# Rebuilt routings in a kernel of two expert layers around an attention block, and a later load of some second weights

## The chip, the cores and the metric

One core of one Trainium2 chip. The metric is the device time of one execution in microseconds. The kernel before was run three times: 213.69, 214.22 and 214.76, median 214.22. One further execution was profiled.

## What is computed

The input `x` holds 4 batches of 512 tokens of width 128, so 2048 tokens. Three steps follow each other, each on a layer-normalised `x`:

```python
x = x + 0.5 * ffn(layernorm(x))      # router + 8 experts, top 1
x = x + attn(layernorm(x))           # linear attention, then a table-gelu MLP of width 512
x = x + 0.5 * ffn(layernorm(x))      # the same experts again

def ffn(x):
    logits = x @ router_W + router_b                 # 8 experts
    probs  = softmax(logits); top1 = argmax(probs)
    h = relu(x @ W1[e] + b1[e])                      # 128 -> 512, e = top1
    y = h @ W2[e] + b2[e]                            # 512 -> 128
    return probs[top1] * y
```

The reference computes all experts for all tokens. The kernel computes only the chosen one.

## The kernel before, in words

**Routing.** A routing finds the expert of each token, gives each token a place in a list sorted by expert, and cuts the list into tiles of 128 rows. Each expert's part is rounded up to whole tiles, so there are at most `NT` = 23 tiles. A tile has a *code*, its expert times 16 (`TPE`) plus its number within the expert. The chain of the first routing, by line:

- SP (SyncE) loads `x` in four groups (L374), then `rw`, `rb`, `eb1r`, the second biases, all first weights (L379, 2048 KB) and the eight second weights, one DMA of 256 KB each (L381). It then issues four small loads of `gb` (L386). TensorE waits for `rw` and `rb` together (L1022) before it averages the router's weights.
- VectorE takes statistics (L1208, L1211) of each group. GpSimd makes `rstd` and, for groups 0 and 1, `shift` (`normaliser`, L497 to L512).
- TensorE turns `x` (L858), ScalarE copies it out (L655), TensorE multiplies by the centred router weights (L889). `pick` on VectorE (L1229 to L1245, seven instructions for two groups) makes the one-hot `oh`.
- Between and behind the two `pick`s VectorE normalises groups 2 and 3 (L1218, `renormalise`). ScalarE normalises groups 0 and 1 (L701) and stores all four groups to DRAM, `xn_scratch` (L706).
- `ranks` (L898 to L912) counts on TensorE; `route` on VectorE goes on: `hits` (L1272), `tcol` (L1274, L1276), `v` and `pos` (L1279 to L1283), `qf`, `steps`, `inv` (L1286 to L1289), `rf` (L1292), `code` (L1296), `inq` (L1299) and sixteen `inr` (L1258, `row_hits`). TensorE's part of it is `tile_list` (L919 to L923) and `sources` (L968). VectorE writes the result as `srcu` (L1264), the row number of each list place.
- GpSimd turns `code` into the list of experts `eid` (L554 to L556). SP and TensorE read the list into registers (L326, 23 registers each).
- GpSimd waits for the stores of `xn_scratch` and for `srcu`, then gathers each tile by an indirect DMA into `Xg` (L549).

**Experts.** For each tile SP copies the expert's first weights inside SBUF to `ewc_own` (L390, 322 KB). `load_weights(k)` for k of 3 and more waits until TensorE has turned tile k-4, or the first one. TensorE turns the tile (`turn`, L978), multiplies by the first weights (`up`, L985) and by the second (`down`, L1000). ScalarE applies the relu (L681), VectorE copies and adds (L1349, L1355). In the first layer the order on TensorE is turn 0, turn 1, up 0, and then for each tile k: turn k+2, up k+1, down k. All eight second weights are waited for (`w2_in`) before turn 0. From tile 8 on SP also stores results (L394) and loads one attention weight for each tile (L409).

**Second routing.** It is incremental: `pick(1, b)` and `place(b)` run batch by batch during the last MLP, and GpSimd scatters the rows with their statistics into `row_scratch` (L609, four DMAs for each batch). Before batch b's `rstd` (L501) GpSimd scatters two of the four parts of batch b-1. After the last batch come `hits`, `tcol` (L1331, L1333), `steps` (L1335), `inv` (L1336), `code` (L1339), the list of codes (L1340) and the list of experts (L1341 to L1343). SP and TensorE read the experts' list, ScalarE reads the first eight codes and loads eight tiles of rows (L332). SP reads the codes when it reaches tile 8; from there on it loads rows for tile k after `out_done` of tile k-8, the landing of its output store (L617, GpSimd).

**Warm-up products.** `keep_warm(n)` (L842) issues n products of ones on TensorE with no result that is used.

The list read and the row load are:

```python
def load_list(eng, table, most):
    return nc.values_load_multi_w_load_instructions(table, [eng.engine], min_val=0, max_val=most, ...)[1]
for k in range(NT):                     # SP, second layer
    if k == UNROLL:                     # 8
        sp.wait_ge(codes_ready, 1)
        codes = load_list(sp, lists[0:1, 1, :], CODES - 1)
        for g in range(NG):
            sp.wait_ge(scattered[g], 16 * GT)
```

## Time and profile before

| | |
|---|---|
| median of 3 runs | 214.22 us (213.69 to 214.76) |
| the profiled execution, own time | 215.13 us |
| its span on the core | 213.4 us |
| TensorE busy | 190.5 us, 89% |
| VectorE, ScalarE, GpSimd busy | 124.7, 107.5, 119.8 us |
| mean granted TensorE clock | 0.968 |
| DMA | 40.26 MB, mean 189 GB/s |

In the profile PE is TensorE's matmuls and PEld its weight loads, DVE is VectorE, ACT ScalarE, POOL GpSimd, SP SyncE; a q behind the name is the engine's queue, which issues DMAs and reads registers. All times in rows are microseconds from the start of the span, if not marked ns. PEclk is the granted TensorE clock as a share of full speed: 1.00 is 2.4 GHz, 0.50 is 1.2 GHz. TensorE's busy share holds the warm-up products.

### The profile page before, as it was taken

The page shows a single profiled execution, that of the slowest core. Times are in us where ns is not written, and L with a number is a line of the kernel's source. Part 1 is how long each engine was busy: PE and PEld are TensorE (multiplying, and loading weights), DVE is VectorE, ACT ScalarE, POOL GpSimd, SP SyncE. Part 2 cuts the span into 40 slices and gives each one's busy share as a digit, 9 for nine tenths or more (in the row PEclk, how much of TensorE's full clock was granted, in tenths as well). Part 3 has the DMA queues.
Part 4 walks back from the last instruction along what each step waited for, and adds up shares of the span by engine and source line. Part 5 has one row for each costly group of instructions (what it writes and reads, how often), then busy time and mean ns, then how long its engine had stood idle before and what let it go on. Part 6 is the DMA issues. An engine that isn't in the chain of part 4 may idle for free.

```text
span 213.4 us, 4550 instructions
## 1 busy us (share of the span) xinstructions
PE 190.5 (89%) x1414; PEld 159.3 (75%) x1414; DVE 124.7 (58%) x528; ACT 107.5 (50%) x316; POOL 119.8 (56%) x186
## 2 busy tenths in 40 slices
PE   5997839999999888888989999989698999899992
PEld 2763339999999876677775769679335999899991
DVE  4688811222222773988797674777433776677762
ACT  2630004665556479747878863510301666466670
POOL 7872277755586445743777531857770245355544
PEclk9998875999999999999999999999969999999999
DMA  5999688779996231299990000011119838586700
GB/s 160 228 388 342 170 286 318 226 249 327 264 285 187 59 80 37 77 418 416 415 420 20 2 3 0 27 40 43 40 54 324 305 103 283 182 278 203 258 25 0
DMA packets 29752, 40.26 MB, mean 189 GB/s; under 512 B 4229, under 2 KB 20392, under 8 KB 28704
## 3 DMA queue, kind: packets, MB, share of 16 engines
q1 hardware_dynamic: 23968, 33.58, 44.3%
q0 software_dynamic: 2496, 4.76, 8.7%
q10 hardware_dynamic: 3264, 1.62, 2.6%
q8 instruction: 12, 0.20, 0.4%
q14 instruction: 12, 0.10, 0.1%
HBM read 10.78 MB, written 14.46 MB: 118 GB/s over the span
## 4 chain that ended last, share of the span: by engine, by line
PE 54%; POOL 13%; DMA 11%; DVE 9%; issue 8%; ACT 2%; SPq 1%; POOLq 0%; DVEq 0%
PE bank L985 14%; PE bank L1000 13%; PE bank L1122 6%; PE bank L842 5%; PE bank L1138 5%; POOL xnT L570 5%; DMA xnT<-slot_scratch,posu 3%; DMA eqrq<-row_scratch 2%; PE bank L978 2%; POOL h L579 2%; DMA Xg<-xn_scratch,srcu 2%; DMA out_dram<-ysb,eqrq 2%; DMA rb<-in_L_ffn_router_b_dram 2%; POOL ew L627 1%; PE bank L889 1%
## 5 line engine op out<-in xcount | busy, mean ns | idle before, releaser
L681 ACT ACTIVATE hT<-bank,ewc_own 128x128 f32<-128x128 f32 x184 | 52.6, 369 | 63.8 <-PE bank L985 62.9
L985 PE MATMUL bank<-xT,ewc_own 128*128 128x128 f32 x368 | 50.8, 283 | 0.6 <-DVE xT L1349 0.6
L1000 PE MATMUL bank<-ew,hT 128*128 x368 | 49.6, 279 | 0.0
L985 PEld LDWEIGHTS bank<-xT,ewc_own 128*128 128x128 f32 x368 | 46.6, 198 | 1.5 <-issue 1.0
L1000 PEld LDWEIGHTS bank<-ew,hT 128*128 128x128 f32 x368 | 45.6, 195 | 0.4 <-issue 0.4
L617 POOL DMA_INDIRECT out_dram<-ysb,eqrq x23 | 22.5, 979 | 29.5 <-DVE ysb L1359 26.2
L549 POOL DMA_INDIRECT Xg<-xn_scratch,srcu x23 | 22.0, 957 | 15.3 <-PE bank L978 7.5
L842 PE MATMUL bank<-ones_bf 128*128 128x512 bf16 x83 | 25.8, 446 | 3.4 <-POOL ident L466 2.6
L1355 DVE TENSOR_TENSOR ysb<-bank,ewc_own 128x128 f32<-128x128 f32 x23 | 6.7, 290 | 28.9 <-PE bank L1000 28.8
L609 POOL DMA_INDIRECT row_scratch<-pay,posu x16 | 15.8, 987 | 10.9 <-DVE posu L1317 7.6
L570 POOL DMA_INDIRECT xnT<-slot_scratch,posu x16 | 15.4, 962 | 10.5 <-DMA slot_scratch<-ysb 6.7
L1349 DVE COPY xT<-bank 128x128 f32<-128x128 f32 x46 | 13.0, 283 | 8.9 <-PE bank L978 8.9
L842 PEld LDWEIGHTS bank<-ones_bf 128*128 128x128 bf16 x83 | 8.4, 115 | 12.7 <-issue 6.6
L978 PE MATMUL bank<-ident,Xg 128*128 128x128 f32 x46 | 13.2, 288 | 4.8 <-DMA Xg<-xn_scratch,srcu 3.3
L1138 PE MATMUL bank<-w,actT 128*128 128x128 f32 x128 | 16.3, 278 | 0.0
L1138 PEld LDWEIGHTS bank<-w,actT 128*128 128x128 f32 x128 | 15.1, 192 | 0.0
L1122 PE MATMUL bank<-h1T,w 128*128 128x512 f32 x32 | 14.4, 592 | 0.0
L776 ACT ACTIVATE actT<-ewc_own 128x512 f32<-128x512 int16 x16 | 9.3, 622 | 8.0 <-DVE ewc_own L1545 8.0
L1359 DVE SCALAR_TENSOR_TENSOR ysb<-bank,gate,ysb 128x128 f32<-128x128 f32 x23 | 8.1, 351 | 8.6 <-PE bank L1000 7.6
L978 PEld LDWEIGHTS bank<-ident,Xg 128*128 128x128 f32 x46 | 6.7, 147 | 6.2 <-DMA Xg<-xn_scratch,srcu 2.5
L1368 DVE TENSOR_SCALAR Xg<-eqrq 128x128 f32<-128x128 f32 x23 | 7.7, 339 | 6.3 <-DMA eqrq<-row_scratch 6.2
L1122 PEld LDWEIGHTS bank<-h1T,w 128*128 128x128 f32 x32 | 5.8, 190 | 5.7 <-issue 5.5
(226 smaller groups left out, 296.8 us busy)
## 6 DMA issues: line engine op xcount, KB each, us to landing
ewc_own<-ew SPq DMA_DIRECT2D x46, 322.0 KB, 4.0
row_scratch<-xn SPq DMA_DIRECT2D x8, 1024.0 KB, 10.6
ew<-in_L_ffn_W_dram SPq DMA_DIRECT2D x1, 2048.0 KB, 11.8
ew<-in_L_ffn_W_dram SPq DMA_DIRECT2D x8, 256.0 KB, 7.7
slot_scratch<-ysb SPq DMA_DIRECT2D x23, 64.0 KB, 2.6
eqrq<-row_scratch SPq DMA_DIRECT2D x15, 70.0 KB, 2.3
x<-in_L_attn_x_dram SPq DMA_DIRECT2D x4, 256.0 KB, 3.8
xn_scratch<-xn ACTq DMA_DIRECT2D x4, 256.0 KB, 6.9
```

Source lines behind the costliest of these rows:

```text
L549: g.indirect_dma_start(out=Xg[:, k % UNROLL, :], out_offset=None, in_=xn_scr, in_offset=bass.IndirectOffsetOnAxis(ap=srcu[:, k:k + 1], axis=0)
L570: g.indirect_dma_start(out=Yg[:, t, :], out_offset=None, in_=here, in_offset=bass.IndirectOffsetOnAxis(ap=posu[:, t:t + 1], axis=0)).then_ ...
L609: g.indirect_dma_start(out=row_scr, out_offset=bass.IndirectOffsetOnAxis(ap=posu1[:, t:t + 1], axis=0), in_=pay[:, t, :], in_offset=None). ...
L617: g.indirect_dma_start(out=out_rows, in_=ysb[:, k, :], in_offset=None, bounds_check=TOK - 1, oob_is_err=False, out_offset=bass.IndirectOff ...
L681: last = A(hT[:, t.slot, c * P:(c + 1) * P], up_bank(k, c)[:, c * P:(c + 1) * P], ACT.Relu, scale=0.5 if m else 1.0, bias=ewc[t.ahead][:, ...
L842: mm(bank[2][:, :], ones_bf[:, :], bc(ones_bf[:, :].unsqueeze(1), [P, 4, P]), start=True, stop=True)
L978: nc.tensor.transpose(bank[t.parity][:, 0:P], Xg[:, t.ahead, :], ident[:, :]).then_inc(xg_T, 1)
L985: last = mm(up_bank(k, c)[:, c * P:(c + 1) * P], ewc[t.ahead][:, c * P:(c + 1) * P], xT[:, t.slot, :], start=True, stop=True)
L1000: last = mm(bank[4 + t.parity][:, 0:D], hT[:, t.slot, c * P:(c + 1) * P], ew[:, bass.ds(e[k], 1), W2_AT + c * D:W2_AT + (c + 1) * D].squee ...
L1122: mm(hidden_bank(c)[:, :], w1[:, c * P:(c + 1) * P], h1T[:, b % 2, :], start=True, stop=True).then_inc(u_ps, 1)
L1138: last = mm(row_bank(b, j)[:, j * P:(j + 1) * P], actT[:, b % 2, c, j * P:(j + 1) * P], w2[:, c, :], start=c == 0, stop=c == FC - 1)
L1349: v.tensor_copy(xT[:, t.slot, :], bank[t.parity][:, 0:P]).then_inc(xT_ready, 1)
```

## The change

In words, by place:

- **Layout.** Partition p of `x` holds four neighbouring tokens of a batch, 2 KB in one piece of DRAM, where it held four tokens 128 apart. `xn_scratch`, `token1` and the token numbers in `pay` follow.
- **Front.** ScalarE's queue loads `rw` first of all; `rb` has a semaphore of its own, waited for by VectorE ahead of `pick`. ScalarE takes all four `xnT` first, then normalises groups 0, 1 and 3; GpSimd normalises group 2. VectorE normalises none and makes the four `shift`s.
- **First routing.** Constants that VectorE added are put into PSUM by TensorE ahead of time (`whole`, `add_step`, `tileid`, `ecapb`). Of the 16 `inr` VectorE makes 9, GpSimd 3 and ScalarE 4, in two instructions each. The expert list comes from an integer shift on VectorE. SP reads codes instead of experts and works out the expert in registers. TensorE reads its list before `sources`.
- **Weights.** SP issues five of the eight second weights in front, and the last three behind the first tile's `load_weights`. The wait for all eight moves to down 0. The four `gb` loads move behind the attention weights, at tiles 14 to 17.
- **Experts.** In both layers TensorE's order is turn 0, warm-up, up 0, turn 1.
- **Second routing.** The same in PSUM. One scatter instead of two goes ahead of the last `rstd`. SP reads all codes at the start; SP and ScalarE wait until TensorE has read its list (`experts_loaded`) before they issue DMAs. ScalarE loads five tiles of rows, SP the other three at tile 3.

```diff
-    x_v = x_d.rearrange("b (t p) d -> p (b t) d", p=P)
+    x_v = x_d.rearrange("b (p j) d -> p b j d", j=GT)
...
+        def load_w2(eng, experts):
+            for e in experts:
+                eng.dma_start(ew[:, e, W2_AT:EW]..., ew2_d[e, :, :]...).then_inc(w2_in, 16)
...
-            for e in range(NE):
-                sp.dma_start(ew[:, e, W2_AT:EW]..., ew2_d[e, :, :]...).then_inc(w2_in, 16)
+            load_w2(sp, range(NE - W2_LATE))
...
-            sp.wait_ge(eid_ready, 1)
-            experts = load_list(sp, eid[0:1, 0:NT], NE - 1)
+            sp.wait_ge(whole_ready, 1)
+            codes = load_list(sp, codei[0:1, 0:NT], NE * TPE - 1)
...
-                load_weights(t, experts[k])
+                load_weights(t, expert_of(codes[k]))
+                if k == 0:
+                    load_w2(sp, range(NE - W2_LATE, NE))
...
-            sp.wait_ge(list_ready, 1)
-            experts = load_list(sp, lists[0:1, 0, :], NE - 1)
+            sp.wait_ge(codes_ready, 1)
+            codes = load_list(sp, lists[0:1, 0:NT], CODES - 1)
             sp.wait_ge(b2_halved, 1)
+            sp.wait_ge(experts_loaded, 1)
...
-                if k == UNROLL:
-                    sp.wait_ge(codes_ready, 1)
-                    codes = load_list(sp, lists[0:1, 1, :], CODES - 1)
+                if k == FIRST:
                     for g in range(NG):
                         sp.wait_ge(scattered[g], 16 * GT)
+                    for n in range(SURE, UNROLL):
+                        load_rows(sp, Tile(n), codes[n])
...
+            for t in range(POOL_ROWS * GT, (POOL_ROWS + 1) * GT):      # GpSimd, POOL_ROWS = 2
+                last = g.tensor_scalar(xn[:, t, :], x[:, t, :], mv[:, t, 0:1], rstd[:, t, 0:1], ALU.subtract, ALU.mult)
+            last.then_inc(xn_by_pool, 1)
+            pool.wait_ge(rf_ready, 1)
+            for t in range(T - ROWS_BY_ACT - ROWS_BY_POOL, T - ROWS_BY_ACT):
+                g.tensor_scalar(inr[:, t, :], rowid[:, :], rf[:, t:t + 1], token1[:, t:t + 1], ALU.is_equal, ALU.mult
+                                ).then_inc(inr_by_pool, 1)
...
+                ahead_of = GT // 2 if b + 1 < B else 1
-                scatter_rows(b - 1, range(GT // 2))
+                scatter_rows(b - 1, range(ahead_of))
                 normaliser(LN_AT["m1", b] - 1)
...
-            take_xn(0, 0)
-            take_xn(0, 1)
+            for g in range(NG):
+                take_xn(0, g)
             renormalise(0)
-            take_xn(0, 2)
-            take_xn(0, 3)
             renormalise(1)
-            for g in range(BY_ACT):
-                store_xn(g)
+            store_xn(0)
+            store_xn(1)
+            renormalise(3)
+            store_xn(3)
+            store_xn(POOL_ROWS)
             exponentials()
-            for g in range(BY_ACT, NG):
-                store_xn(g)
+            row_hits()
...
+            act.wait_ge(experts_loaded, 1)
             for k in range(SURE):
                 load_rows(act, Tile(k), codes[k])
-            act.wait_ge(scattered[NG - 1], 16 * GT)
-            for k in range(SURE, UNROLL):
-                load_rows(act, Tile(k), codes[k])
...
-            keep_warm(8)
+            keep_warm(4)
             ranks()
+            tile_list()
             keep_warm(2)
-            tile_list()
-            keep_warm(WARM_ROUTE // 2)
-            sources()
-            keep_warm(WARM_GATHER // 2)
             pe.wait_ge(eid_ready, 1)
             e = load_list(pe, eid[0:1, 0:NT], NE - 1)
-            keep_warm(2)
-            pe.wait_ge(w2_in, 16 * NE)
+            sources()
+            keep_warm(10)
             experts(0, e)
...
-            keep_warm(5)
+            keep_warm(8)
             ranks1(NG - 1)
             tile_list1()
-            keep_warm(WARM_ROUTE // 2)
+            keep_warm(4)
             pe.wait_ge(list_ready, 1)
-            e = load_list(pe, lists[0:1, 0, :], NE - 1)
-            keep_warm(12)
+            e = load_list(pe, lists[0:1, NT:2 * NT], NE - 1)
+            mm(bank[2][:, 0:P], ones_bf[:, :], ones_bf[:, :], start=True, stop=True).then_inc(experts_loaded, 1)
+            keep_warm(8)
             experts(1, e)
...
             pick(0, 0, 2)
-            renormalise(2)
-            pick(0, 2, 2)
-            renormalise(3)
+            first_shift(2)
             dve.wait_ge(eb1_T, 1)
             v.tensor_copy(ew[:, :, B1_AT:B2_AT], bank[7]...).then_inc(ebias_ready, 1)
+            pick(0, 2, 2)
+            first_shift(3)
             route()
```

Both `code` chains on VectorE:

```diff
-                v.tensor_tensor(out=code[:, :], in0=bank[6][:, 0:NT], in1=tileid[:, :], op=ALU.add
-                                ).then_inc(code_ready, 1)
+                v.tensor_scalar(codei[:, :], bank[6][:, 0:NT], NE * TPE - 1.0, None, ALU.min).then_inc(whole_ready, 1)
+                dve.wait_ge(whole_ready, 1)
+                v.tensor_scalar(eid[:, :], codei[:, :], TPE_BITS, None, ALU.arith_shift_right).then_inc(eid_ready, 1)
...
-                link(v.tensor_tensor(out=code[:, :], in0=bank[6][:, 0:NT], in1=tileid[:, :], op=ALU.add))
-                v.tensor_scalar(lists[:, 1, :], code[:, :], CODES - 1.0, None, ALU.min).then_inc(codes_ready, 1)
-                link(v.tensor_scalar(eidf[:, :], code[:, :], 1.0 / TPE, 0.5 / TPE - 0.5, ALU.mult, ALU.add))
-                link(v.tensor_scalar(eidf[:, :], eidf[:, :], MAGIC, MAGIC, ALU.add, ALU.subtract))
-                v.tensor_scalar(lists[:, 0, :], eidf[:, :], NE - 1.0, None, ALU.min).then_inc(list_ready, 1)
+                link(v.tensor_scalar(codei[:, :], bank[6][:, 0:NT], NE * TPE - 1.0, None, ALU.min))
+                v.tensor_scalar(lists[:, NT:2 * NT], codei[:, :], TPE_BITS, None, ALU.arith_shift_right).then_inc(list_ready, 1)
+                v.tensor_scalar(lists[:, 0:NT], bank[6][:, 0:NT], CODES - 1.0, None, ALU.min).then_inc(codes_ready, 1)
```

## Rows read from the trace of the kernel before

**Rows 1.** The page: busy us of the engines, share of the span, instructions.
```profile
PE 190.5 (89%) x1414; PEld 159.3 (75%) x1414; DVE 124.7 (58%) x528; ACT 107.5 (50%) x316; POOL 119.8 (56%) x186
```

**Rows 2.** The chain that ended last: start, us, what.
```profile
3.50 3.57 DMA rb<-in_L_ffn_router_b_dram
...
12.63 1.11 DVE xn L1218 x4
...
19.57 3.49 PE bank L842 x8
...
26.46 3.70 DMA Xg<-xn_scratch,srcu
...
91.49 2.27 POOL h L579 x4
```

**Rows 3.** The timeline, first routing: start, us, engine, line.
```profile
7.36 1.65 ACT L701 ACTIVATE xn<-x,shift,rstd 128x128 f32<-128x128 f32 x4
...
10.94 0.23 DVE L1229 TENSOR_TENSOR lg<-bank,rstd 128x64 f32<-128x64 f32 x1 [0.66 <-DVE mv L1211]
...
16.46 0.15 DVE L1272 COPY hits<-bank 128x1 f32<-128x1 f32 x1
...
19.68 0.18 DVE L1296 TENSOR_TENSOR code<-bank,tileid 128x23 f32<-128x23 f32 x1
...
20.35 3.21 DVE L1258 TENSOR_SCALAR inr<-rowid,rf,token 128x128 f16<-128x128 f16 x14
...
23.84 0.18 DVE L1264 TENSOR_SCALAR srcu<-bank 128x23 uint32<-128x23 f32 x1 [0.28 <-PE bank L968]
...
24.91 1.25 POOL L549 DMA_INDIRECT Xg<-xn_scratch,srcu  x1 [3.53 <-DVE srcu L1264]
```

**Rows 4.** Line 326, the reads of a list into registers: ns min/median/max, starts.
```profile
L326 SPq TENSOR_LOAD <-lists x2: 2017/3934/5852, 157.5 to 167.2; - x2
L326 PEldq TENSOR_LOAD <-eid x1: 2282/2282/2282, 23.6 to 23.6; - x1
```

**Rows 5.** Windows of 2.5 us: busy by engine, granted clock, DMA share, GB/s.
```profile
17.50:20.00 2.50, 1.96 (x12) 0.83 (x11) 2.29 (x12) 0.00 (x0) 0.06 (x1) 0.90 1.15 341
22.50:25.00 2.50, 2.46 (x25) 1.25 (x23) 2.18 (x8) 0.00 (x0) 0.09 (x1) 0.92 0.84 206
...
32.50:35.00 2.50, 2.50 (x12) 2.50 (x13) 0.29 (x1) 1.44 (x6) 1.88 (x2) 0.50 1.03 373
```

**Rows 6.** Line 706, the stores of `xn_scratch`.
```profile
L706 ACTq DMA_DIRECT2D xn_scratch<-xn x4: 366/410/490, 10.1 to 16.5; - x4
...
DMA to landing us min/median/max: 6.6/6.9/7.4
```

**Rows 7.** Line 381, the second weights.
```profile
L381 SPq DMA_DIRECT2D ew<-in_L_ffn_W_dram x8: 1241/1733/3037, 6.1 to 20.1; - x8
```

**Rows 8.** The timeline, first layer: turn of tile 2, down of tile 0.
```profile
32.42 0.48 PE L978 MATMUL bank<-ident,Xg 128*128 128x128 f32 x1
...
34.39 1.92 PE L1000 MATMUL bank<-ew,hT 128*128 x8
```

**Rows 9.** The timeline, second routing and its first tile.
```profile
149.44 0.38 DVE L1613 BATCH_NORM_AGGREGATE pay<-stat 128x2 f32<-128x6 f32 x4
149.57 0.96 POOL L609 DMA_INDIRECT row_scratch<-pay,posu  x1 [0.31 <-issue]
...
157.32 0.18 DVE L1343 TENSOR_SCALAR lists<-eidf 128x23 int32<-128x23 f32 x1
...
159.67 7.50 SPq L390 DMA_DIRECT2D ewc_own<-ew  x8
...
163.18 0.97 PEld L985 LDWEIGHTS bank<-xT,ewc_own 128*128 128x128 f32 x8 [0.29 <-DMA ewc_own<-ew]
```

**Rows 10.** The chain that ended last, rows of tile 11.
```profile
177.83 4.97 DMA eqrq<-row_scratch
```

**Rows 11.** The waits from 163 us on: us in total, times, longest us.
```profile
DVE Xg L1368 <- DMA eqrq<-row_scratch: 2.5, 2, 1.7
```

More of the change, by code:

```diff
@@ L328, in load_list, with within, expert_of @@
                 skip_runtime_bounds_check_because="the engine that makes the table clamps all of it to this range")[1]
+        def within(value, most):
+            return nc.s_assert_within(value, min_val=0, max_val=most, skip_runtime_bounds_check_because=
+                                      "codes are clamped to 0 to 128, and 128 is taken as 127")
+        def expert_of(code):
+            return within(within(code - (code >> (TPE_BITS + 3)), NE * TPE - 1) >> TPE_BITS, NE - 1)
         def load_rows(eng, t, code):
```

292 lines of the change are left out of this document (164 added, 128 removed).

## The prediction

> **What bounds the kernel now.** I read the page first: TensorE is busy 89% of the span [rows 1], but that holds the warm-up products, so its share tells little. The chain of waits tells more. Through both expert layers it runs on TensorE, tile after tile, and the diff leaves that work alone. It leaves TensorE in the two routings. In the first the chain names `rb` as what ended the wait at 3.50 + 3.57 = 7.07 us, then VectorE's normalising, 1.11 us for four rows, then 3.49 us of warm-up products, then the gather of tile 1 [rows 2]. The warm-up products are no cause: they fill the time in which VectorE makes 14 `inr` in 3.21 us, the last ready at 23.56 [rows 3], and `sources` needs all of them. So the timeline of VectorE is the view to cost this change from. The stage ends with the gathers, of which tile 0's starts at 24.91 [rows 3], and TensorE runs without gaps from the turn of tile 2 at 32.42 [rows 8].
>
> In the second routing the first `up` starts at 163.18 and its wait was ended by the landing of the weights that SP issued at 159.67, 3.5 us before; SP issued them 2.2 us after the list's end at 157.50 [rows 9], and 2.0 us of that is the list read [rows 4].
>
> **First routing, part by part.** The profiled execution took 215.13, 0.91 over the median of 214.22; I work out differences on its rows and take them from the median.
>
> - Front: VectorE waited for `rw` and `rb`, which TensorE needed together. `rw` now goes first on ScalarE's queue. Also five warm-up products of 0.44 us (3.49 for eight [rows 2]) go ahead of the first turn instead of seven, 0.9 us. `pick` starts at 10.94 now [rows 3]; with four groups of statistics on end and two small shifts between them I get 9.8. Gain 1.1.
> - Between the `pick`s one normalising of 1.11 [rows 2] goes, a shift and the bias copy, some 0.2 each, come. Behind the second `pick` the other 1.11 and the copy go, but then the wait is TensorE's answer. `hits`, at 16.46 [rows 3], comes at 14.05: gain 2.4.
> - One instruction of `tcol` (0.14) and two warm-up products ahead of `tile_list` go; of VectorE's chain behind the ranks the addition of `ecap` (0.28, a quarter of the 1.11 in [rows 2], which has as many elements) and that of `steps` (0.15). The four constants come from TensorE, ahead of `oh`, where it idles. `code`, at 19.68 [rows 3], comes at 16.7: gain 3.0.
> - Ahead of `inq` there is one instruction more, 0.2: gain 2.8.
> - `inr`: VectorE makes 7 more, 7 x 0.23 (3.21 / 14) = 1.6 us, done at 19.3. GpSimd makes 3; its nearest row is 2.27 for four rows [rows 2], 0.57 each, done at 18.2 if nothing holds it. ScalarE makes 4 in 8 instructions; its nearest row is 1.65 for four [rows 3], 0.41 each. It comes free at 17.0, behind its third normalising, two stores and the exponentials, so 17.0 + 3.3 + 0.1 = 20.4. ScalarE's are the last. Against 23.56 the gain is 3.15.
> - TensorE's list read moves ahead of `sources`, and everything on TensorE queues behind it. It took 2.28 [rows 4]; from 17.1 it ends at 19.4, covered by ScalarE's `inr` by 1.0 us. GpSimd's three instructions for `eid` leave; nothing waits on them at the end.
> - `srcu` at 20.7 to 20.9 instead of 24.02; the gather's own start, 0.9 behind it [rows 3], stays.
> - The gather also needs the four stores. The last two now go out at 15.7 and 16.2, hardly earlier than the 16.5 of [rows 6], because group 3's shift is late and GpSimd needs 2.27 for group 2. With the landing of [rows 6], 7.4, the last would be there at 23.6: 2.8 late. Against that stand pieces of 2 KB instead of 512 B and 768 KB less in front of them, 2.2 us at 341 GB/s [rows 5]. I take 4.8 for the landing, 21.0, about even with `srcu`, and charge 0.15. Gather 0 starts at 21.9: **gain 3.0**, ends 1.0 and 4.0.
> - Second weights: five DMAs in front, three behind the first tile's weights. SP reads its list from 16.9 to about 19.0, then issues at 19.2 what it issued at 26.1; the three land some 4 us later, by 24.5. The gathers of tiles 0 to 2 run beside them as they ran beside weight loads, 3.70 for tile 1 [rows 2]. Cost 0 while the three land ahead of `down` 0, which was at 34.39 [rows 8] and would be at 30 to 31; past that each microsecond is lost. The four `gb` loads come at tiles 14 to 17, one DMA each on SP's queue, where the attention weights stood at tiles 8 to 13; nothing but the later attention waits for them: 0.
> - `up` 0 ahead of turn 1 fills a wait for the gather; the next wait, tile 2's gather, stays last: 0. From 32.50 to 35.00 TensorE ran at clock 0.50 [rows 5]. It will sit idle there again, so I take the same; if the clock stayed up, half of that stretch, 1.2 us, would come back.
>
> **Second routing.**
>
> - Statistics are done at 149.82, GpSimd's second scatter held it until 150.53 [rows 9]. With one scatter ahead, `rstd` starts 0.7 earlier, and `pick` with it. The moved scatters end where they did: they gate only tiles 5 and later.
> - One instruction in `tcol`, one in `steps` go (0.3), but the warm-up products between hold TensorE: 0.2.
> - The list needs three instructions fewer, about 0.8. SP waits for the codes, made last: ready 1.45 earlier than 157.50 [rows 9], 156.05. The read ends at 158.1. The added wait, `experts_loaded`, ends with TensorE's own read (ready 155.9, plus 2.3, plus one product), 158.4. SP's first weights go at 158.5 instead of 159.67, 1.15 earlier, and land 3.5 later at 162.0. Behind SP's wait stand all weights, behind ScalarE's the rows of tile 0: those go at 158.4, land about 2 later, with slack.
> - TensorE: 8 warm-up products from 158.4 take 1.8 us at full clock and 3.5 at the lower one, then turn and 2 more, so `up` 0 is free at 161 or 163.1. Gain 1.15 or 0.1; I take **0.9**.
> - Tiles 8 on: SP's second read took 5.85 [rows 4], from 167.2 to 173.05; tile 8's rows and weights could not go out before, and 9 to 11 crowded behind. Tile 11's rows landed after 4.97 [rows 10], and VectorE waited 2.5 us for rows in two waits [rows 11], of which the gaps on TensorE show about half, 1.3. The read is gone from there. The round trip of store and reload stays, so I take half of the 1.3: **0.6**, ends 0 and 1.3.
>
> Sum: 3.0 + 0.9 + 0.6 = 4.5, so 214.22 - 4.5 = **209.7 us**. Its own range is 207 to 212.
>
> **A rule beside a row.** 23 registers took 2.28 us [rows 4], 99 ns each, while the DMA share in that window was 0.84 and falling [rows 5]; the same read at a full share took 5.85, 254 ns each. The Trainium skill, Runtime: NRT & Kernel Launch, section Instruction fetch mechanics, states about 200 ns for each register. By that figure, as an estimate, the read would take 4.6, end at 21.7 and leave 1.2 of the 3.0, total 211.5; the reads of the second routing, all about 2.0, speak against it.
>
> **The rivals.**
>
> 1. *The slow list read.* At 17.1 the DMA engines may still be full: from 17.50 to 20.00 the share was 1.15 [rows 5]. For it: the one read made under full DMA took 5.85. Against: five DMAs in front, not eight, end some 2 us sooner. The read ends at 22.95, `sources` takes 0.9, `srcu` is at 24.1: the first routing gains nothing, the second its 1.5. Time 212.7.
> 2. *The stores decide.* The last lands at 23.6, as now, and gather 0 goes at 24.0. Gain 0.9 + 1.5: 211.8. For it: the landings of [rows 6], all alike whatever was ahead; against it: larger pieces.
> 3. *Nothing measurable.* Slow read, and TensorE at 0.50 through the first tiles of the second layer, as it has fewer warm-up products after a longer idle time; that costs about 0.9 for each `up` or `down`, half of the 1.92 that `down` 0 took at the lower clock [rows 8]; one of them and the lost head start of 0.3 take the 1.5 down to 0.3. 213.9.
> 4. *Slower: the late second weights hold down 0.* SP's read is slow (22.8), then the tile's weights and three DMAs, each as slow to issue as the slowest, 3.04 [rows 7]: issued by 32.8, and landing as late as a store did in that crowd, 7.4 [rows 6], 40.2. `down` 0 would start there instead of at 34.39 [rows 8]: 5.8 lost, 1.5 gained, 218.5. It decides from a landing at 37.0 on (34.39, the 1.5, and 1.1 more). Against it: the backlog that made those DMAs slow is gone by then.
>
> **How the numbers follow.** The forecast gets 0.58, the rivals 0.17, 0.12, 0.07 and 0.06. About 0.5%, 1.1 us, is what a measurement of this kernel can tell from no change. Faster: 0.58 + 0.12 and nearly all of rival 1, 0.16, so 0.86. Same: rival 3 and the rest of rival 1, 0.08. Slower: 0.06. The range leaves out rivals 3 and 4 and the best corner: upper end 213.1, rival 1 with the second routing's lower end; lower end 206.9, first routing 4.0, second 1.15 and 1.3, and part of the clock's 1.2.
>
> **What would show it.** In the changed profile `hits` near 14.0, `code` near 16.7, `srcu` near 20.8, the first gather near 21.9 and ended by `srcu` or a store; TensorE's list read near 2.3 us; turn of tile 2 near 29.4; the first weights of the second layer 1.15 sooner than now, counted from the end of batch 3's statistics; no list read behind tile 7. A list read of 4 us or more at 17, or a wait of `down` 0 for `ew`, would make the prediction wrong, and a lower clock in the second layer's first tiles would take the 0.9.

## The result and the profile after

| | before | after |
|---|---|---|
| median of 19 runs each | 213.41 us (212.25 to 214.82) | 215.74 us (213.52 to 219.59) |
| ratio | | 1.0064, 95% interval 1.0036 to 1.0092 |
| the profiled execution, own time and span | 215.13, 213.4 us | 214.22, 212.5 us |
| mean granted TensorE clock in it | 0.968 | 0.939 |

The change makes the kernel slower by 0.6%. The forecast was 209.7 us. The ratios here and below leave out runs that took over 1.5% more than the fastest of their kernel, which the medians keep (five of the changed kernel's 19 are such runs), so the medians lie 2.3 us apart and the ratio says 1.4 us. Note which executions the profiles show: that of the kernel before is slower than all 19 of its runs, that of the changed kernel is the fifth fastest of its 19. So the two traces, read side by side, show the change 0.9 us ahead, and the medians show it 2.3 us behind. The traces tell where time moved; only the medians tell how much is left.

The page of the changed kernel: busy us of each engine, and the granted clock in 40 slices.

```profile
PE 186.4 (88%) x1403; PEld 157.8 (74%) x1403; DVE 120.1 (57%) x512; ACT 112.2 (53%) x328; POOL 123.5 (58%) x187
...
PEclk9965578999999999999999999999966999999998
```

VectorE has 4.6 us less than in [rows 1], ScalarE and GpSimd 4.7 and 3.7 more, as planned. The clock row has a hollow of three slices at 6, 5 and 5, from 10.6 to 26.6 us.

Its timeline in the first routing (start, us, engine, line), to be laid beside [rows 3]:

```profile
13.37 3.15 POOL L568 TENSOR_SCALAR xn<-x,mv,rstd 128x128 f32<-128x128 f32 x4
14.26 0.16 DVE L1343 COPY hits<-bank 128x1 f32<-128x1 f32 x1 [0.31 <-PE bank L954]
15.67 1.21 ACTq L749 DMA_DIRECT2D xn_scratch<-xn  x2
17.72 2.59 POOL L573 TENSOR_SCALAR inr<-rowid,rf,token 128x128 f16<-128x128 f16 x3 [1.21 <-DVE rf L1357]
18.17 0.17 DVE L1362 TENSOR_SCALAR codei<-bank 128x23 int32<-128x23 f32 x1
19.03 1.65 ACT L760 ACTIVATE inr<-off_row,token,minus_token 128x128 f16<-128x128 f16 x4
20.79 0.57 SPq L405 DMA_DIRECT2D ewc_own<-ew  x1
21.41 1.80 SPq L364 DMA_DIRECT2D ew<-in_L_ffn_W_dram  x3
21.72 0.18 DVE L1335 TENSOR_SCALAR srcu<-bank 128x23 uint32<-128x23 f32 x1 [0.99 <-PE bank L1041]
23.26 1.25 POOL L591 DMA_INDIRECT Xg<-xn_scratch,srcu  x1 [1.46 <-issue]
28.51 0.33 PE L1051 MATMUL bank<-ident,Xg 128*128 128x128 f32 x1 [2.56 <-DMA Xg<-xn_scratch,srcu]
34.29 0.27 PE L1051 MATMUL bank<-ident,Xg 128*128 128x128 f32 x1
```

`hits` is 2.2 us earlier than before, the list of codes 1.5, `srcu` 2.1, gather 0 1.65. But gather 0 takes 5.2 us to land, and turn 0, at 28.51, is *later* than in the kernel before, where it stood at 27.91. Still the turn of tile 4 is 2.0 us earlier (36.19 for 38.22). The windows show why: engines' busy time, then the granted clock. First the changed kernel, then the kernel before.

```profile
12.75:26.25 13.50, 9.83 (x62) 4.93 (x62) 7.70 (x32) 4.88 (x13) 10.08 (x22) 0.50 1.01 321
26.25:29.75 3.50, 0.91 (x5) 0.56 (x6) 0.29 (x1) 0.00 (x0) 2.65 (x3) 0.99 0.70 227
29.75:33.25 3.50, 3.24 (x16) 2.87 (x16) 0.51 (x2) 1.14 (x4) 2.83 (x3) 0.52 0.75 258
33.25:36.75 3.50, 3.50 (x34) 3.50 (x34) 0.84 (x4) 2.29 (x8) 2.58 (x4) 1.00 0.95 336
```

```profile
12.50:19.50 7.00, 5.46 (x49) 3.07 (x47) 6.06 (x30) 0.31 (x1) 2.53 (x15) 1.00 1.11 360
19.50:23.00 3.50, 3.50 (x14) 1.30 (x13) 3.46 (x16) 0.00 (x0) 1.27 (x3) 0.52 1.15 343
29.75:36.50 6.75, 6.27 (x28) 5.98 (x29) 0.74 (x3) 2.29 (x8) 4.92 (x7) 0.50 0.97 358
```

TensorE runs at its lower level from 12.6 to 26.3 us, where the kernel before had it for one stretch of 3.5 us. In return the second low stretch lasts 3.5 us, not 6.75: in 33.25 to 36.75 it makes 34 products, where the kernel before made 19. So the lead at tile 4 comes of the clock, not of the earlier list. A later trace of the kernel before (its second list moved, which touches nothing here) bears this out: its second low stretch lasted 3.4 us instead of 6.8, and its tile 4 was turned at 36.44. In the seven traces with the new routing on chips of this speed, this one among them, it is at 35.62 to 36.69.

The second routing of the changed kernel, to be laid beside [rows 9]:

```profile
147.42 0.38 DVE L1673 BATCH_NORM_AGGREGATE pay<-stat 128x2 f32<-128x6 f32 x4
153.41 0.18 DVE L1403 TENSOR_SCALAR lists<-codei 128x23 int32<-128x23 int32 x1
159.39 0.26 PE L1256 MATMUL bank<-ones_bf 128*128 128x128 bf16 x1 [5.27 <-issue]
159.45 3.56 PE L896 MATMUL bank<-ones_bf 128*128 128x512 bf16 x8
160.00 2.11 SPq L405 DMA_DIRECT2D ewc_own<-ew  x3
163.60 1.13 PE L1058 MATMUL bank<-xT,ewc_own 128*128 128x128 f32 x8
```

and its list reads, as in [rows 4]:

```profile
L336 SPq TENSOR_LOAD <-codei x1: 2045/2045/2045, 18.4 to 18.4; - x1
L336 PEldq TENSOR_LOAD <-eid x1: 2288/2288/2288, 18.6 to 18.6; - x1
L336 PEldq TENSOR_LOAD <-lists x1: 5712/5712/5712, 153.6 to 153.6; - x1
L336 SPq TENSOR_LOAD <-lists x1: 1939/1939/1939, 153.7 to 153.7; - x1
L336 ACTq TENSOR_LOAD <-lists x1: 732/732/732, 153.7 to 153.7; - x1
```

This is the main finding. The list of experts is made 1.9 us sooner against the statistics (5.99 behind 147.42; before 7.88 behind 149.44), and then TensorE needs 5.7 us to read it. SP and ScalarE, which have their codes after 1.9 and 0.7 us, stand at `experts_loaded` until 159.7. `up` 0 starts 16.18 us behind the statistics; before it was 13.74. From there to the end the changed kernel takes 48.9 us, before 50.2: the gap near tile 11 is gone. In sum the traces say 2.0 - 2.4 + 1.3 = 0.9.

### The profile page after: what moved, and what is told of

It reads as the page before. It is cut to its first block, busy times and chain, and to the rows that moved or that the text cites. A ratio compares the mean times of both kernels' runs of the same rounds, so it can differ in the third digit from the quotient of the medians.

```text
span 212.5 us, 4528 instructions
## 1 busy us (share of the span) xinstructions
PE 186.4 (88%) x1403; PEld 157.8 (74%) x1403; DVE 120.1 (57%) x512; ACT 112.2 (53%) x328; POOL 123.5 (58%) x187
## 4 chain that ended last, share of the span: by engine, by line
PE 60%; POOL 14%; issue 9%; DVE 6%; DMA 6%; ACT 2%; POOLq 0%; DVEq 0%
PE bank L1058 18%; PE bank L1075 16%; PE bank L1192 6%; PE bank L1208 6%; POOL xnT L609 5%; PE bank L896 4%; DMA Xg<-xn_scratch,srcu 2%; DMA xn_scratch<-xn 2%; PE bank L1051 2%; POOL h L618 2%; DVE stat L1279 2%; DMA slot_scratch<-ysb 2%; POOL xn L568 1%; POOL ew L666 1%; PE bank L1157 1%
## 5 line engine op out<-in xcount | busy, mean ns | idle before, releaser
L1058 PE MATMUL bank<-xT,ewc_own 128*128 128x128 f32 x368 | 50.2, 281 | 1.2 <-DVE xT L1410 1.2
L1075 PE MATMUL bank<-ew,hT 128*128 x368 | 48.8, 276 | 0.0
L1058 PEld LDWEIGHTS bank<-xT,ewc_own 128*128 128x128 f32 x368 | 45.8, 196 | 2.8 <-issue 2.8
L1075 PEld LDWEIGHTS bank<-ew,hT 128*128 128x128 f32 x368 | 44.8, 192 | 0.4 <-issue 0.4
L896 PE MATMUL bank<-ones_bf 128*128 128x512 bf16 x58 | 20.7, 490 | 2.7 <-POOL ident L486 2.7
L609 POOL DMA_INDIRECT xnT<-slot_scratch,posu x16 | 15.4, 960 | 10.5 <-DMA slot_scratch<-ysb 6.9
L1208 PE MATMUL bank<-w,actT 128*128 128x128 f32 x128 | 16.3, 278 | 0.0
L1051 PE MATMUL bank<-ident,Xg 128*128 128x128 f32 x46 | 12.7, 281 | 3.2 <-DMA Xg<-xn_scratch,srcu 2.6
L896 PEld LDWEIGHTS bank<-ones_bf 128*128 128x128 bf16 x58 | 6.3, 120 | 9.2 <-issue 4.9
## 6 DMA issues: line engine op xcount, KB each, us to landing
row_scratch<-xn SPq DMA_DIRECT2D x8, 1024.0 KB, 10.6
ew<-in_L_ffn_W_dram SPq DMA_DIRECT2D x1, 2048.0 KB, 12.6
```

The source lines that it names most:

```text
L609: g.indirect_dma_start(out=Yg[:, t, :], out_offset=None, in_=here, in_offset=bass.IndirectOffsetOnAxis(ap=posu[:, t:t + 1], axis=0)).then_ ...
L896: mm(bank[2][:, :], ones_bf[:, :], bc(ones_bf[:, :].unsqueeze(1), [P, 4, P]), start=True, stop=True)
L1051: nc.tensor.transpose(bank[t.parity][:, 0:P], Xg[:, t.ahead, :], ident[:, :]).then_inc(xg_T, 1)
L1058: last = mm(up_bank(k, c)[:, c * P:(c + 1) * P], ewc[t.ahead][:, c * P:(c + 1) * P], xT[:, t.slot, :], start=True, stop=True)
L1075: last = mm(bank[4 + t.parity][:, 0:D], hT[:, t.slot, c * P:(c + 1) * P], ew[:, bass.ds(e[k], 1), W2_AT + c * D:W2_AT + (c + 1) * D].squee ...
L1208: last = mm(row_bank(b, j)[:, j * P:(j + 1) * P], actT[:, b % 2, c, j * P:(j + 1) * P], w2[:, c, :], start=c == 0, stop=c == FC - 1)
```

## The experiments

**The theory.** Two reads took 5.7 and 5.85 us, all others of 23 registers 1.9 to 2.3. Both slow ones read a list that begins at byte 92 of its tile (23 entries of 4 bytes); the quick ones begin at byte 0. In the kernel before ScalarE too read from byte 92, eight codes in 2.02 us; that is 253 ns for each, as for TensorE (5.71 / 23 = 248). The prediction had laid the 5.85 on full DMA engines; from 153.6 to 159.3 the DMA engines of the changed kernel were busy 0.17 of the time. *Theory:* the place of the list makes the read slow. *Rivals:* the reads of three engines at one time get in each other's way; the second read on TensorE is slow by its position in the program; the late second weights or the new waits cost the time.

The kernels were timed in five groups, each on one chip and beside the kernel before (the expectations say "call" for such a group). The chips were of two kinds: the kernel before took 230.66, 224.55 and 229.65 us in the first, second and fifth group, 213.29 and 213.59 in the third and fourth. The second and fifth were on one and the same chip. Only kernels of one group are compared by time; the durations of list reads agree on all chips.

### First group: the list at byte 128

```diff
-        lists = sb("lists", [P, 2 * NT], i32)
+        lists = sb("lists", [P, 64], i32)
...
-            e = load_list(pe, lists[0:1, NT:2 * NT], NE - 1)
+            e = load_list(pe, lists[0:1, 32:32 + NT], NE - 1)
...
-                v.tensor_scalar(lists[:, NT:2 * NT], codei[:, :], TPE_BITS, None, ALU.arith_shift_right).then_inc(list_ready, 1)
+                v.tensor_scalar(lists[:, 32:32 + NT], codei[:, :], TPE_BITS, None, ALU.arith_shift_right).then_inc(list_ready, 1)
```

> The changed kernel with the second list of the last routing moved from byte 92 of its tile to byte 128; nothing else. Theory A (a read of a list that starts at byte 92 goes at about 250 ns a register, one that starts at byte 0 at 90): TensorE's read of the experts takes 2.3 us instead of 5.7, the first weights of the second layer go out some 3.4 us sooner, and the kernel is 2.5 to 3.5 us faster than the changed kernel, so about 1 to 2 us faster than the kernel before. Rival B (three engines that read at once, or the scatters beside them, slow the read): it stays at 5.7 and the time at the changed kernel's, 0.6% over the kernel before.

TensorE's read took 2.10 us, so for the read the rivals on position and on three readers fall: nothing else was changed. The time was 229.9 (ratio to before 1.013, 1.002 to 1.023). A kernel 1 to 2 us faster than before had been expected; on this chip it is slower.

The kernel before, its list of codes moved to byte 128 in the same way:

> The kernel before with the codes' list moved from byte 92 to byte 128. Theory A: SP's read ahead of tile 8 takes about 2.0 us instead of 5.85, and ScalarE's of eight codes under 1 us instead of 2.0; the gaps on TensorE around tile 11 shrink, and the kernel is 0.5 to 1.5 us faster. Rival B (that read was slow because the DMA engines were full of weights): 5.85 stays, and the time too.

The list reads of that kernel:

```profile
L326 SPq TENSOR_LOAD <-lists x2: 1962/2490/3017, 172.8 to 182.2; - x2
L326 ACTq TENSOR_LOAD <-lists x1: 749/749/749, 172.3 to 172.3; - x1
```

SP's read at tile 8 fell from 5.85 to 3.02 at the same spot, under the same weight traffic. So of the 3.8 us by which it stood out in [rows 4], about 2.8 come of the place and 1.0 of the traffic. The time was 231.06 (0.994, 0.986 to 1.002), no difference clear of the noise.

All second weights in front again (`W2_LATE = 0`) in the changed kernel:

> The changed kernel with all eight second weights issued in front again. If the late issue is worth something, the stores of xn_scratch land later here and the first gather starts up to 1 us later: +0.5 to +1 us against the changed kernel. Rival: the three late DMAs and the weights beside them are why the first gather took 5.2 us to land; then it lands in about 3 us here and the kernel is up to 1 us faster than the changed one.

Gather 0 began at 23.81, 0.55 later than in the first trace of the changed kernel, its wait ended by the landing of `xn_scratch`, and turn 0 came 4.57 us behind it. The time was 234.47 us (1.030, 1.018 to 1.042). The changed kernel was not timed in this group (in the next, on another chip, it stands at 1.015), so the price of the late second weights is not measured; nothing here makes them a cause of the loss.

The changed kernel without both waits on `experts_loaded`:

```diff
-            sp.wait_ge(experts_loaded, 1)
...
-            act.wait_ge(experts_loaded, 1)
```

> The changed kernel without the two waits for experts_loaded: SP and ScalarE issue weights and rows while TensorE still reads its list. Theory A: TensorE's read stays at 5.7, so the first product stays where it is, but rows and weights have landed by then; 0 to 0.7 us faster than the changed kernel. Rival B (other traffic slows the read): the read grows beyond 6.5 us and the kernel is 1 us or more slower.

```profile
L336 PEldq TENSOR_LOAD <-lists x1: 7595/7595/7595, 174.0 to 174.0; - x1
```

The read grew from 5.7 to 7.6 us with the row and weight copies running beside it, and `up` 0 came 18.23 us behind the statistics, where the changed kernel has 16.18. The time was 234.6 (1.029, 1.018 to 1.040), again without the changed kernel beside it. So by the trace the waits do not make the loss, they limit it; by the time it is not shown.

### Second group: repeats, warm-ups behind, the old lists swapped

The changed kernel as it is, and the aligned one again:

> The changed kernel itself, beside the others of this call on the same chip. Theory A (the read that starts at byte 92 is what costs): TensorE's read of the experts takes 5.7 us and the kernel is 2.5 to 4.5 us slower than the aligned one. Rival B (the aligned kernel was faster by chance of its chip): no difference over 1 us.

> The aligned kernel of the first experiment again, as the base for the next one and against the changed kernel on the same chip. Theory A: 2.5 to 4.5 us faster than the changed kernel, and 0 to 3 us faster than the kernel before. Rival B: the same as the changed kernel.

229.17 and 228.10 us, both 1.015 of before (1.010 to 1.021; 1.010 to 1.020). The reads were 5.72 and 2.12, and turn 0 came 15.4 and 11.9 us behind the statistics, but the ratios are the same: 2.5 to 4.5 us had been expected, and on this chip the quicker read is not seen in the time. In all ten traces from these slower chips, of old and new kernels, TensorE stands for 2.2 to 6.3 us near 40 us and for 1.5 to 4.7 us at one to three places between 72 and 95; the profile names "issue" or "remote", on TensorE itself or on the ScalarE or VectorE that it waits for. This may hide the gain, which is not shown.

More warm-up products around the first list (8 ahead of the ranks, 2 ahead of `inv`, 9 behind the list), on the aligned kernel:

> The aligned kernel with warm-up products back in the first routing: 8 ahead of ranks instead of 4, 2 ahead of inv instead of 1, and 9 behind tile_list instead of 2. Theory C (the first routing gained 1.5 us less than worked out because TensorE ran at clock 0.50 through it): the granted clock stays at 1.00 through most of 10 to 22 us, code comes 0.7 to 1.3 us sooner, and the kernel is 0.5 to 1.5 us faster than the aligned one. Rival D (the products made ahead in PSUM stand in the way, whatever the clock): code comes at most 0.3 sooner, the time stays.

It did not help: the clock fell at 11.0 us, the first added products came at 13.4, and it stayed at 0.50 to 24.6, though TensorE was busy without a break from 12 to 24. Products added behind the fall did not bring the clock back. The six runs, 224.5 to 234.7 us with a median of 230.5, scatter too much for a verdict on the time.

The kernel before with its two lists exchanged, so that the experts stand at byte 92:

```diff
-                v.tensor_scalar(lists[:, 1, :], code[:, :], CODES - 1.0, None, ALU.min).then_inc(codes_ready, 1)
+                v.tensor_scalar(lists[:, 0, :], code[:, :], CODES - 1.0, None, ALU.min).then_inc(codes_ready, 1)
...
-                v.tensor_scalar(lists[:, 0, :], eidf[:, :], NE - 1.0, None, ALU.min).then_inc(list_ready, 1)
+                v.tensor_scalar(lists[:, 1, :], eidf[:, :], NE - 1.0, None, ALU.min).then_inc(list_ready, 1)
...
```

The reads on SP, ScalarE and TensorE follow their lists.

> The kernel before with only the places of its two lists swapped, as the change has them: codes at byte 0, experts at byte 92. Theory A: SP's and TensorE's reads of the experts take 5.7 to 5.9 us, the reads of the codes 0.7 to 3, the first weights of the second layer go out 3.7 us later, and the kernel is 2 to 3.5 us slower than before. Rival B: no change in time.

```profile
L326 ACTq TENSOR_LOAD <-lists x1: 740/740/740, 165.9 to 165.9; - x1
L326 SPq TENSOR_LOAD <-lists x1: 5056/5056/5056, 166.5 to 166.5; - x1
L326 PEldq TENSOR_LOAD <-lists x1: 5826/5826/5826, 166.5 to 166.5; - x1
```

This is the change's mistake put into the kernel before, alone: TensorE's read goes from 2.3 to 5.8 us and SP's of the same list from 2.0 to 5.1, no tile is moved, and ScalarE's codes, now at byte 0, take 0.74. With the first group this settles from both sides what makes the reads slow. Which property of byte 92 it is, no run tells; only 0, 92 and 128 were tried. The time goes from 224.55 to 231.8, ratio 1.035 (1.031 to 1.039). That is more than the 2 to 3.5 us expected and more than the read explains: `up` 0 comes 19.51 us behind the statistics, where the kernel before with its list at byte 128 (first group) has 14.58. The rest is open.

### Third group: the first routing

SP holds the weights of tiles 1 to 7 until gather 0 has landed, and GpSimd makes its masks behind gather 7:

```diff
                 if k == 0:
                     load_w2(sp, range(NE - W2_LATE, NE))
+                    sp.wait_ge(g_in[0], 16)
...
```

> The changed kernel with the experts' list at byte 128, and two edits in the first routing: SP issues tile 0's weights and the late w2 as before, then waits for gather 0 to land before it issues the weights of tiles 1 to 7, and GpSimd makes its masks and memsets behind gather 7 instead of in front of gather 0. If the 5.2 us that gather 0 took to land in the changed kernel (3.0 in the kernel before) comes of the weight copies that SP now issues ahead of it, gather 0 lands in about 3 us and turn 0 comes some 2 us earlier against the list of codes, plus up to 0.5 us from GpSimd: turn 0 about 8.0 us behind codei instead of 10.3, and the time falls by 1 to 2.5 us against the aligned kernel in the same call. If the landing is slow for another reason (the indirect reads themselves, or the xn stores), it stays near 5 us and the time stays or rises by what tile 1's weights come late.

The warm-up products of the kernel before in the front:

> The aligned kernel with the warm-up matmuls of the kernel before in the front: 7 at the start, 2 in each of the four groups, 8 ahead of the ranks, 2 ahead of inv (instead of 5, 1 in two groups, 4 and 1). If TensorE's half clock from 12.6 us on comes of the warm-ups that the change took out of the front, the clock stays at 1.00 to about 19 us as in the kernel before, codei follows hits in 3.3 us instead of 3.9, and the sum of half-clock stretches before 46 us falls from 17 or 20 us to about 10, the mean clock from 0.92 to 0.94 or more. If the half clock has another cause, it begins at 11 to 13 us again. Time: 0 to 1.5 us less than the aligned kernel in the same call by the first, the same or 0.5 us more by the second.

Both:

> Both of the edits above together on the aligned kernel. If each acts by itself, the gains add: 2 to 3 us less than the aligned kernel in the same call, which would bring it to or below the kernel before. If only the gather's landing matters, it is as fast as the kernel with the gather first alone; if only the clock does, as the one with the old warm-ups.

The reference:

> The aligned kernel again, as the reference for the three others on this chip: gather 0 landing about 5 us after its issue, the half clock from 11 to 13 us on, and TensorE's read of the experts' list 2.1 us. Against the kernel before: 1.01 to 1.015 if the chip is like those of the earlier calls, 0.985 to 1.0 if it is like the one on which the change was first timed, since there 3.6 us of the list read would come off 215.7.

| | median us | ratio to before (interval) | gather 0, issue to turn 0 |
|---|---|---|---|
| gather first | 212.40 | 0.9936 (0.990 to 0.997) | 24.34 to 28.57 |
| old warm-ups | 212.71 | 0.9913 (0.988 to 0.995) | 23.83 to 28.35 |
| both | 214.0 | none given | 24.16 to 28.12 |
| aligned | 212.33 | 0.9944 (0.991 to 0.998) | 23.58 to 28.11 |

On this chip the aligned kernel beats the kernel before. Holding the weights back did not do what was expected: the landing fell from 4.5 to 4.2 us (4.0 with both), not to 3. In all traces with the new routing it took 4.0 to 5.2, in four of the old one 3.0 to 3.5. Tile 0's weights and the late second weights still go ahead of it here; whether these or the new layout of `xn_scratch` slow it, no run separates.

The old warm-ups did what was expected of the clock. Windows of that kernel:

```profile
6.10:12.90 6.80, 6.63 (x54) 5.76 (x53) 4.62 (x32) 5.07 (x12) 5.29 (x14) 1.00 1.00 321
12.90:19.75 6.85, 5.77 (x51) 3.32 (x50) 4.64 (x22) 3.34 (x11) 4.76 (x11) 1.00 1.12 352
19.75:26.50 6.75, 4.38 (x26) 1.77 (x26) 4.10 (x15) 1.93 (x5) 5.07 (x11) 0.50 0.68 208
```

The full clock holds to 19.7 us, the codes follow `hits` in 3.20 us for 3.92, and the mean clock is 0.964. The time shows no gain clear of the noise: the ratio is 0.003 lower than the aligned kernel's, the intervals overlap, and the median is 0.4 us higher. Nor did turn 0 come sooner. In the aligned trace of this group the gather waited for a store, not for `srcu`:

```profile
23.58 1.25 POOL L591 DMA_INDIRECT Xg<-xn_scratch,srcu  x1 [1.85 <-DMA xn_scratch<-xn]
```

Turn 0 comes at 28.1 to 28.6 in all four, whether `hits` was at 14.2 or 16.3.

In the second layer the aligned trace shows a new wait in place of the old:

```profile
156.20 1.89 PE L896 MATMUL bank<-ones_bf 128*128 128x512 bf16 x8
156.60 2.42 ACTq L351 DMA_DIRECT2D eqrq<-row_scratch  x5
156.70 2.09 SPq L405 DMA_DIRECT2D ewc_own<-ew  x3
163.26 4.49 SPq L405 DMA_DIRECT2D ewc_own<-ew  x5
167.18 1.05 PE L1058 MATMUL bank<-xT,ewc_own 128*128 128x128 f32 x7 [1.41 <-DMA ewc_own<-ew]
```

SP issued three tiles' weights at 156.7, then waited 2.4 us for the last scatters, which end when they always did, and tile 3's weights came too late by 1.4. `up` 0 is 11.98 us behind the statistics (changed kernel 16.18). Of these 4.2 us 3.6 are the read; most of the rest goes with the clock, which fell to 0.50 at 156.0 in the changed kernel while TensorE stood in its read (there the eight warm-up products behind it take 3.56 us) and stays at 1.00 here (1.89). But from there to the end it takes 50.6 us, not 48.9: 1.7 of the 4.2 is given back.

### Fourth group: the four versions side by side

No edit; the changed kernel as it is:

> The changed kernel itself, so that it stands beside the others of this call on one chip. In the calls so far TensorE's read of the experts' list took 5.7 us with the list at byte 92 and 2.1 us at byte 128, but the two kernels were timed on a fast chip in different calls (1.0064 and 0.9944 against the kernel before). If the misplaced list is the main cause: about 1.006 again, and 1.0 to 1.3% slower than the aligned kernel of this call. If the sessions differed instead: both within 0.3% of each other.

The aligned kernel, with SP's wait for the scatters two tiles later (`SURE` is 5, `FIRST` is 3):

```diff
-                if k == FIRST:
+                if k == SURE:
                     for g in range(NG):
                         sp.wait_ge(scattered[g], 16 * GT)
```

> The aligned kernel, and SP waits for the scattered rows (and loads the rows of tiles 5 to 7) behind the weights of tile 4, not in front of those of tile 3. In the aligned kernel's trace SP waited 2.4 us there for the last scatter and TensorE then 1.4 us for tile 3's weights, as the scatter's end does not move when the list is read sooner. If that wait is what gives part of the 3.6 us back, TensorE's gap at the up projection of tile 3 goes (turn of tile 4 at one step of 1.9 us behind that of tile 3, not 3.0 to 3.6) and the time falls by 0.7 to 1.5 us against the aligned kernel in this call; if another wait takes its place (rows of tile 5 landing), it falls by under 0.4.

The aligned version of the kernel before:

> The kernel before with its list of codes at byte 128 instead of 92. If the misplaced list costs the kernel before only what SP's 5.85 us read at tile 8 shows (a gap of about 1.3 us on TensorE around tile 11, and ScalarE's read of eight registers, 2.02 against 0.75, which is covered), it is 0.3 to 0.7% faster than the kernel before. If the read at tile 8 is slow for the full DMA engines, as the prediction had it, nothing changes (within 0.2%).

The aligned kernel:

> The aligned kernel, the reference for the others of this call: 0.994 of the kernel before if the last call was typical, PE's list read 2.1 us.

| | median us | ratio to before (interval) |
|---|---|---|
| changed | 215.11 | 1.0032 (0.9998 to 1.0067) |
| aligned | 212.62 | 0.9915 (0.988 to 0.995) |
| aligned, rows late | 212.24 | 0.9916 (0.988 to 0.995) |
| before, aligned | 213.51 | 0.9998 (0.997 to 1.003) |

The place of one list makes 2.5 us between the changed and the aligned kernel, and their intervals do not touch. So on this chip the slow read is what the change loses by: without it the kernel is 0.8% ahead of the kernel before, with it 0.3% behind. The rows waited for late remove the gap (tiles 3 to 5 at steps of 1.9 us, 48.9 us from `up` 0 to the end), but the ratio is that of the aligned kernel: the 0.7 to 1.5 us expected are not there. The kernel before gains nothing measurable from alignment; by the interval at most 0.6 us. Yet its trace, like that of the swapped one, lacks the gap near tile 11: 48.9 us from `up` 0 to the end, and 50.2 before. So in the traces the gap goes with the slow read; why the time does not show it is open (in that trace `up` 0 comes 0.8 later behind the statistics, which may be chance). The aligned kernel's own profiled execution in this group took 372.5 us, and nothing is read from it.

### Fifth group: where the lead goes

```diff
-BACK = {17: (0, 1), 18: (2, 3), 20: (4, 5), 21: (6, 7)}
+BACK = {18: (0, 1), 19: (2, 3), 20: (4, 5), 21: (6, 7)}
```

> The aligned kernel with the rows waited for late, and VectorE's adds of the four tiles of batch 0 that come back from the first expert layer put one tile later (behind tiles 18 and 19 instead of 17 and 18). In the traces VectorE waits for these gathers 0.4 to 0.8 us in the kernel before and up to 2.9 us in kernels with the new first routing, with the copy of the next turned tile behind it, and TensorE then stands for up to 2.7 us. If that is what eats the lead of the new first routing and makes its runs spread, TensorE's wait on xT near 70 us goes below 1 us in the trace and the median falls by 0.5 to 1.5 us against the kernel of this call that lacks the edit, with fewer runs above 214. If the gathers come later still for other reasons, or finish_rstd for batch 0 becomes late instead, the time is the same within 0.3 us.

> The reference of this call for the edit above: the aligned kernel with the rows waited for behind the weights of tile 4. 0.99 to 0.995 of the kernel before, as in the last call (0.9916); TensorE's steps at tiles 3 to 5 of the second layer 1.9 us each.

What led to it is this stretch of the kernel with the rows late, in the fourth group:

```profile
69.21 0.94 POOL L609 DMA_INDIRECT xnT<-slot_scratch,posu  x1 [2.46 <-DMA slot_scratch<-ysb]
70.22 0.61 DVE L1471 SCALAR_TENSOR_TENSOR x<-xnT,gate,x 128x128 f32<-128x128 f32 x2 [2.73 <-DMA xnT<-slot_scratch,posu]
...
71.28 0.27 DVE L1410 COPY xT<-bank 128x128 f32<-128x128 f32 x1
...
71.70 2.05 PE L1058 MATMUL bank<-xT,ewc_own 128*128 128x128 f32 x8 [2.52 <-DVE xT L1410]
```

VectorE's add of a returned tile waits for its gather; the copy of the next turned tile is queued behind it on VectorE; TensorE waits for the copy. TensorE's wait at this place was 0.2 and 0.6 us in two traces of the kernel before, and 0.5, 0.6, 0.9, 1.7, 2.5, 2.7 and 2.7 in seven of the new first routing on the quick chips. In the four with 1.7 us or more the statistics of the second routing come 112.3 to 114.6 us behind the turn of tile 4, in the other three and in both traces of the kernel before 110.8 to 111.6. So the wait is not made up before the second routing. In the two with the longest stretch, 114.4 and 114.6, the granted clock also fell to 0.50 for 3.4 us behind it, at 71.5 and 70.9.

The group fell on a slow chip: 228.4 us with the edit (ratio 0.9993, 0.986 to 1.013), 230.88 without (1.019, 1.010 to 1.027). The medians lie 2.5 us apart, but the intervals overlap, and neither trace of this group shows the wait, with or without the edit; both show the unexplained pauses. So the theory is open: the traces of the other groups show the mechanism, no run shows its price in the time. And the kernel without the edit, 0.8% faster than before in the fourth group, is 1.9% slower here, where 0.5 to 1% less had been expected.

## Why the prediction was wrong

**The step that failed** is the cost of reading a list into registers. The prediction put the 5.85 us in [rows 4] down to full DMA engines, took 2.3 for TensorE's read in the second routing, and so came to a gain of 0.9. The read took 5.71, and the routing lost 2.4. What the prediction did not ask of the two rows is where each list begins; the diff says it in plain sight, for the experts move from `lists[:, 0, :]` to `lists[:, NT:2 * NT]`. Traffic does slow the read, by 1.0 of the 3.8. The Trainium skill, Runtime: NRT & Kernel Launch, section Instruction fetch mechanics, states about 200 ns for each register. That lies between what the traces here show: 82 to 100 ns with the list at byte 0 or 128 and no copies beside it, 220 to 253 ns at byte 92, 330 ns at byte 92 with copies beside it. With the list aligned the routing gains 13.77 - 11.98 = 1.8 up to `up` 0, twice the 0.9.

**The first routing, 3.0 forecast, 2.0 in the trace.** `hits` was right (14.26 for 14.05). Then:

- *`code` at 18.17, not 16.7.* The clock was read from [rows 5] only for tiles; that the change also takes warm-ups out of the front, and that these hold the clock for the ranks, was missed. With them back, 3.20 us instead of 3.92. But the kernel before also has 3.22: the instructions that the prediction took off this chain (0.6) gave nothing even at the full clock.
- *GpSimd's price.* 0.79 us for one `xn` and 0.86 for one `inr`, where 0.57 was taken from another operation with another shape of operands in [rows 2]. Its `inr` ended at 20.31 and its masks at 21.80, just behind `srcu`.
- *The stores.* Taken at 21.0; the last, issued at 16.55, lands after 5.8 us, at 22.3, behind `srcu`, which was ready at 21.90. The gather starts 0.96 later, about the 0.9 that it took behind `srcu` before. Rival 2 was half right: in three other traces the profile itself names the landing of a store as what the gather waited for.
- *The landing of gather 0* had no term at all. It was 3.0 before and 5.2 after, and took the whole gain and 0.6 more. What the prediction charged with 0, the traffic of SP's earlier weights, stands beside it; that it is the cause was not confirmed.
- The 2.0 that the trace does show comes from the clock returning one stretch sooner. The prediction had left this to chance ("1.2 us, would come back"), and it is luck: in other traces of these kernels the low stretches lie elsewhere, and against the later trace of the kernel before (36.44) the lead at tile 4 is 0.25.

**Tile 8 on, 0.6 forecast.** The trace gives 1.3, but the kernel before with its read repaired is not faster (0.9998). The prediction took differences on the trace of one execution, which took 1.7 us more than the median of 19, and subtracted them from a median. What the gap is worth in the median is not shown; by the interval it is 0.6 at most.

**The range.** Its upper end, 213.1, is said to be rival 1 with the second routing's lower end. That would be 214.1; 213.1 is the forecast with its own lower ends, 1.0, 0.1 and 0. The measured 215.74 lies above both.

**The rivals.** The slow list read (0.17) named the right wait, in the wrong routing and for the wrong reason: TensorE's first read took 2.29 us at full DMA share, the second 5.71 at a share of 0.17. The late second weights did not hold `down` 0. Slower, at 0.06, got far too little: a wait moved onto TensorE (the read ahead of two other engines, held by a new semaphore) deserved a rival of its own, at 5.85 - 2.27 = 3.6 us. The clock behind a longer read belongs to it too.

**What was right:** the earlier statistics and list of the second routing, the disappearance of the reads at tile 8, and that a sound version gains, in the third and fourth groups; by its ratios it gains 1.2 to 1.8 us there, not 4.5. In the three groups on slower chips the aligned versions are 1.3 to 1.9% slower than the kernel before, but for the one with the moved adds (0.9993), and no run shows why.

## What to carry to other kernels

Begin every list that an engine reads into registers at the start of its own tile or at byte 128, the offsets that were quick here, and when two rows of one instruction differ by a factor of three, compare their operands before blaming the traffic. Before subtracting a trace's gap from a median, see where the profiled execution stands among the runs. Where a diff removes idle-time products ahead of a chain of small ones, look at the granted clock over that chain and at what the chain's end waits for besides it.

## What was not expected of the hardware

- A read of 23 registers took 1.9 to 2.3 us from byte 0 or 128, on the queues of TensorE and SP, in all five groups. From byte 92 it took 5.7 to 5.8 us on TensorE (five traces) and 5.1 on SP (one). Eight registers took 0.74 to 0.77 and 2.02 us. Two engines' copies beside it added 1.9 us to the slow read on TensorE; weight copies added 0.9 to 1.3 us to SP's quick one (2.94, 3.02 and 3.27).
- A granted clock of 0.50 lasted from 11.0 to 24.6 us while TensorE was busy without a break from 12 us on with warm-up and ranking products; with twelve more warm-up products ahead of the ranks it stayed at 1.00 to 19.7.
- The chips of three groups ran the kernel before 5 to 8% slower than the chips of the others did, with pauses of 2.2 to 6.3 us on TensorE near 40 us and of 1.5 to 4.7 us between 72 and 95 us in all ten traces, and no run here explains them.
